# An attention loop's context products gathered from two visits of 32 passes into one of 64

## The reference

```python
q, k, v = (proj(Wq, bq), proj(Wk, bk), proj(Wv, bv))     # 8 heads of 32
scores = jnp.einsum('bhqd,bhkd->bhqk', q, k) * SCALE
scores = scores * (adj_matrix + bond_matrix)[:, None, :, :]
attn = jax.nn.softmax(scores, axis=-1)
ctx = jnp.einsum('bhqk,bhkd->bhqd', attn, v)
ctx = ctx.transpose(0, 2, 1, 3).reshape(b, seq_len, EMBED_DIM)
return jnp.einsum('bse,fe->bsf', ctx, Wo) + bo
```

## Time and profile before

| | us |
|---|---|
| median of 3 runs | 3239.82 |
| lowest, highest | 3238.65, 3240.64 |
| profiled execution | 3240.96 |
| its span, first to last instruction | 3239.2 |
| TensorE busy | 3078.7 |
| VectorE busy | 2119.0 |
| ScalarE busy | 1710.0 |
| POOL busy | 444.6 |

### The profile page before, as it was taken

The page is one execution under the profiler, slowest core; times in us unless marked ns, Lnnn a source line. Parts: engine busy times, 40 slices in busy tenths (PEclk is TensorE's granted clock), DMA queues, the critical chain, the costliest instruction groups (busy, mean ns, idle before and its releaser), DMA issues.

```text
span 3239.2 us, 71078 instructions
## 1 busy us (share of the span) xinstructions
PE 3078.7 (95%) x28440; PEld 2706.9 (84%) x28440; DVE 2119.0 (65%) x3844; ACT 1710.0 (53%) x2945; POOL 444.6 (14%) x1666
## 2 busy tenths in 40 slices
PE   7999999999999998999989999899998999989999
PEld 6988789887898788987789877898778987789877
DVE  5636976279762797627966279663886538875388
ACT  3425854258442684426844268442784327743277
POOL 0001210012100121001211012111121111211112
PEclk9999999999999999999999999999999999989999
DMA  5022131121311213212133021330213302133020
GB/s 211 26 80 63 48 141 48 58 69 44 138 59 50 66 51 131 79 33 67 47 131 98 16 70 43 129 105 12 68 51 121 105 14 68 53 117 105 17 47 19
DMA packets 145270, 234.51 MB, mean 72 GB/s; under 512 B 12840, under 2 KB 113965, under 8 KB 144941
## 3 DMA queue, kind: packets, MB, share of 16 engines
q1 hardware_dynamic: 144940, 229.96, 22.0%
HBM read 120.86 MB, written 83.89 MB: 63 GB/s over the span
## 4 chain that ended last, share of the span: by engine, by line
PE 84%; DVE 10%; ACT 3%; issue 1%; SPq 1%; POOL 1%; DMA 0%; DVEq 0%; POOLq 0%; ACTq 0%
PE ps L463 15%; PE ps L465 15%; PE ps L464 15%; PE ps L661 14%; PE ps L651 9%; PE ps L679 7%; DVE rsum L1172 2%; PE ps L543 2%; PE ps L597 1%; PE ps L518 1%; DVE xt_lo L1093 1%; PE ps L532 1%; PE ps L692 1%; SPq L366 1%; DVE al_area L1206 1%
## 5 line engine op out<-in xcount | busy, mean ns | idle before, releaser
L1328 DVE CUSTOM_DVE_ANT_0 r<-ps,adjn 128x1024 f32<-128x1024 f32 x512 | 620.7, 1212 | 20.9 <-DVE xr L1364 11.3
L1037 ACT ACTIVATE r<-r,nmax 128x1024 f32<-128x1024 f32 x512 | 585.3, 1143 | 23.7 <-POOL nmax L455 22.6
L463 PE MATMUL ps<-u_hi,t_hi 128*128 128x256 f32 x2048 | 590.3, 288 | 5.3 <-DVE u_lo L1086 4.8
L464 PE MATMUL ps<-u_lo,t_hi 128*128 128x256 f32 x2048 | 581.5, 284 | 0.0
L465 PE MATMUL ps<-u_hi,t_lo 128*128 128x256 f32 x2048 | 581.2, 284 | 0.0
L661 PEld LDWEIGHTS ps<-ident,r 128*128 128x128 f32 x4096 | 461.5, 140 | 116.1 <-issue 77.6
L661 PE MATMUL ps<-ident,r 128*128 128x128 f32 x4096 | 537.0, 274 | 7.4 <-DVE pt L1344 7.2
L1344 DVE COPY pt<-ps 128x512 f32<-128x512 f32 x512 | 353.0, 689 | 93.1 <-PE ps L661 71.3
L463 PEld LDWEIGHTS ps<-u_hi,t_hi 128*128 128x128 f32 x2048 | 394.3, 193 | 9.8 <-DVE u_lo L1086 6.4
L836 ACT ACTIVATE pt<-ps 128x512 f32<-128x512 f32 x512 | 304.2, 594 | 176.0 <-PE ps L661 157.7
L464 PEld LDWEIGHTS ps<-u_lo,t_hi 128*128 128x128 f32 x2048 | 395.0, 193 | 0.0
(11 more groups left out here) (157 smaller groups left out, 5282.4 us busy)
## 6 DMA issues: line engine op xcount, KB each, us to landing
adjn<-in_adj SPq DMA_DIRECT2D x64, 512.0 KB, 3.5
t_spill<-t_hi SPq DMA_DIRECT2D x64, 512.0 KB, 4.1
t_spill<-t_lo SPq DMA_DIRECT2D x64, 512.0 KB, 5.1
t_hi<-t_spill SPq DMA_DIRECT2D x32, 1024.0 KB, 5.3
t_lo<-t_spill SPq DMA_DIRECT2D x32, 1024.0 KB, 8.2
xn<-in_x SPq DMA_DIRECT2D x16, 512.0 KB, 4.6
x_spill<-xn SPq DMA_DIRECT2D x64, 128.0 KB, 1.7
q_stack<-u_hi SPq DMA_DIRECT2D x64, 128.0 KB, 2.4
```

Source lines behind the costliest of these rows:

```text
L463: pe.matmul(dst, a_hi, b_hi, start=first, stop=False, skip_group_check=check)
L464: pe.matmul(dst, a_hi, b_lo, start=False, stop=False, skip_group_check=check)
L1037: act.activation(r[:, s % RSLOTS, :], r[:, s % RSLOTS, :], ACT.Exp, bias=nmax[:, s % 4:s % 4 + 1], accum_out=prow[:, qt % 2, h:h + 1]).the ...
L1328: dve.tensor_tensor_reduce(out=r[:, s % RSLOTS, :], in0=ps[:, 2 * (s % 2):2 * (s % 2) + 2, :].rearrange("p a c -> p (a c)"), in1=adjn[:, q ...
```

## The change

It calls `context` once for each group, at s = 4 grp + 8, with all eight key tiles (64 weight loads and 64 passes), waiting for both engines' copies. `ctx_half` goes; VectorE's copy waits for `ctx_done`. The spread moves one step earlier, to 8 qt + 11, the output product one step later, to 8 qt + 17. With the output, these move one step later: VectorE's residual sum and statistics, POOL's `norm_tile`, ScalarE's normalisation. The diff:

```diff
--- before.py
+++ after.py
@@ -253,7 +253,6 @@
         p_full = sem("p_full")
         p_act = sem("p_act")
         p_dve = sem("p_dve")
-        ctx_half = sem("ctx_half")
         ctx_done = sem("ctx_done")
         rp_ready = sem("rp_ready")
         rbc_full = sem("rbc_full")
@@ -435,9 +434,9 @@
                 layer_norm(b, 0)
                 for layer in (1, 2):
                     layer_norm(b, layer)
-                for u in range(UNITS + 13):
-                    if u >= 20 and (u - 20) % H == 0 and (u - 20) // H < NT:
-                        norm_tile(b, 3, (u - 20) // H)
+                for u in range(UNITS + 14):
+                    if u >= 21 and (u - 21) % H == 0 and (u - 21) // H < NT:
+                        norm_tile(b, 3, (u - 21) // H)
                     if u >= 16 and (u - 16) % H == 0 and (u - 16) // H < NT - 1:
 
                         qt = (u - 16) // H
@@ -662,24 +661,22 @@
                                             r[:, u % RSLOTS, (TPH * half + t) * P:(TPH * half + t + 1) * P], ident)
                     last.then_inc(p_full, 1)
 
-            def context(b, grp, part):
+            def context(b, grp):
 
                 qt, g = divmod(grp, 2)
-                if part == 0:
-                    pe.wait_ge(p_dve, nth(b, UNITS, G * grp + G))
-                    if grp == 0:
-                        pe.wait_ge(pr_free, nth(b, PR_UNITS, PR_UNITS))
-                    elif g == 0:
-                        pe.wait_ge(c_raw, nth(b, NT, qt))
-                else:
-                    pe.wait_ge(p_act, nth(b, UNITS, G * grp + G))
-                for kt in range(TPH * part, TPH * (part + 1)):
+                pe.wait_ge(p_dve, nth(b, UNITS, G * grp + G))
+                if grp == 0:
+                    pe.wait_ge(pr_free, nth(b, PR_UNITS, PR_UNITS))
+                elif g == 0:
+                    pe.wait_ge(c_raw, nth(b, NT, qt))
+                pe.wait_ge(p_act, nth(b, UNITS, G * grp + G))
+                for kt in range(NT):
                     for hh in range(G):
                         h = g * G + hh
                         last = pe.matmul(ps[HD * hh:HD * (hh + 1), 6, g * P:(g + 1) * P],
                                          xn[:, kt, h * HD:(h + 1) * HD], p_half(grp * G + hh, kt // TPH)[:, kt % TPH, :],
                                          start=(kt == 0), stop=(kt == NT - 1), tile_position=(0, HD * hh))
-                last.then_inc(ctx_done if part else ctx_half, 1)
+                last.then_inc(ctx_done, 1)
 
             def spread_denominators(b, qt):
 
@@ -821,14 +818,13 @@
                         project_pairs(b, "values", W_V, xt_wait(b, 3), range(s, s + 1))
                     if LAG <= s < UNITS + LAG:
                         transpose_p(b, s - LAG)
-                    for part in range(2):
-                        grp, late = divmod(s - 7 - 2 * part, G)
-                        if late == 0 and 0 <= grp < 2 * NT:
-                            context(b, grp, part)
-                    if s >= 12 and (s - 12) % H == 0 and (s - 12) // H < NT:
-                        spread_denominators(b, (s - 12) // H)
-                    if s >= 16 and (s - 16) % H == 0 and (s - 16) // H < NT:
-                        output(b, (s - 16) // H)
+                    grp, late = divmod(s - 8, G)
+                    if late == 0 and 0 <= grp < 2 * NT:
+                        context(b, grp)
+                    if s >= 11 and (s - 11) % H == 0 and (s - 11) // H < NT:
+                        spread_denominators(b, (s - 11) // H)
+                    if s >= 17 and (s - 17) % H == 0 and (s - 17) // H < NT:
+                        output(b, (s - 17) // H)
 
 
         @block.scalar
@@ -1017,9 +1013,9 @@
                     act.activation(qk_place(part, u_hi, qk0_hi), ps[:, PR + n % 2, :], ACT.Identity,
                                    bias=cols[:, 2 + m, ft:ft + 1]).then_inc(qk_hi, 1)
                 stacks_copied(range(G, 4 * G, 2))
-                for s in range(UNITS + 14):
-                    if s >= 21 and (s - 21) % H == 0 and (s - 21) // H < NT:
-                        normalise(b, 3, (s - 21) // H)
+                for s in range(UNITS + 15):
+                    if s >= 22 and (s - 22) % H == 0 and (s - 22) // H < NT:
+                        normalise(b, 3, (s - 22) // H)
                     if LAG <= s < UNITS + LAG:
                         u = s - LAG
                         if u == 0:
@@ -1316,7 +1312,7 @@
                                              scalar=cols[:, 2 + m, ft:ft + 1], in1=f32(qk_place(part, u_hi, qk0_hi)),
                                              op0=ALU.add, op1=ALU.subtract).then_inc(pr_free, 1)
                 stacks_copied(range(G + 1, 3 * G + 2, 2))
-                for s in range(UNITS + 13):
+                for s in range(UNITS + 14):
                     if s < UNITS:
                         qt, h = divmod(s, H)
                         dve.wait_ge(s_full, nth(b, UNITS, s + 1))
@@ -1340,7 +1336,7 @@
                                 dve.wait_ge(stacked[g], nth(b, 16 * 6, 16 * 6))
                         dve.wait_ge(p_full, nth(b, 2 * UNITS, 2 * u + 1))
                         if u >= P0SLOTS:
-                            dve.wait_ge(ctx_half, nth(b, 2 * NT, (u - P0SLOTS) // G + 1))
+                            dve.wait_ge(ctx_done, nth(b, 2 * NT, (u - P0SLOTS) // G + 1))
                         dve.tensor_copy(p_half(u, 0).rearrange("p t q -> p (t q)"), ps[:, TP, :]).then_inc(p_dve, 1)
                     if s >= 8 and (s - 8) % H == 0 and (s - 8) // H < NT:
                         qt = (s - 8) // H
@@ -1357,8 +1353,8 @@
                     if s == H * (NT - 1) + 15:
                         dve.wait_ge(c_hi_ready, nth(b, NT, NT))
                         rest(c_lo[:, :, :], c_f[:, :, :], c_hi[:, :, :], c_ready)
-                    if s >= 17 and (s - 17) % H == 0 and (s - 17) // H < NT:
-                        qt = (s - 17) // H
+                    if s >= 18 and (s - 18) % H == 0 and (s - 18) // H < NT:
+                        qt = (s - 18) // H
                         dve.wait_ge(o_full, nth(b, NT, qt + 1))
                         dve.wait_ge(xr_biased, nth(b, NT, qt + 1))
                         dve.tensor_tensor(xr[:, qt % 2, :], ps[:, 7, 0:F], xr[:, qt % 2, :],
@@ -1366,8 +1362,8 @@
                         dve.wait_ge(h_sum, nth(b, NT, qt + 1))
                         if qt == NT - 1:
                             dve.sem_inc(drained, 1)
-                    if s >= 18 and (s - 18) % H == 0 and (s - 18) // H < NT:
-                        tile_stats(b, 3, (s - 18) // H)
+                    if s >= 19 and (s - 19) % H == 0 and (s - 19) // H < NT:
+                        tile_stats(b, 3, (s - 19) // H)
 
 
 # ---- launch: one core; inputs and outputs as the reference has them ----
```

## The result

| | us, median | lowest, highest | ratio to before, 95% interval |
|---|---|---|---|
| before | 3239.83 | 3238.65, 3240.64 | |
| after | 3307.31 | 3302.14, 3313.65 | 1.0209 (1.0191 to 1.0228) |

The change made the kernel 67.5 us slower. 3304 us was forecast. The profiled execution took 3308.51 us, its span 3306.7.

A forecast was written before the change was run, and what follows sets the result against it. TensorE's work fills visit steps; light steps take 1.48 us singly, 1.75 in a row at VectorE's pace. Per element +7.6 - 0.8 + 1.2 gives +8.0, 64 us for eight: 3304 us, range 3264 to 3324.

The forecast's parts named there:

- The mechanism: Attention loop: a single light step between visits takes 1.48 us; from the second in a row VectorE's mask-copy order makes it 1.75.
- The price of the merged visit: Context visit of 64 passes on TensorE: 1.89 us, against 2.02 for two visits of 32.
- The 0.41 saved per group: TensorE time per merged visit: 0.13 us from the visit itself, 0.18 at transposes, 0.10 at scores; lower bound 0.31.
- The group with xr and the spread: Steps 0 to 3 modulo 8, with visit, output, residual sum and spread: 9.34 us visit to visit, spread hidden with 0.27 spare.
- t1 to t4: Starts of the transposes in steps with s = 1 to 4 modulo 8: forecast 2.46, 4.51, 5.99, 8.37 us.
- ScalarE's lateness: Rbc and normalisation before ScalarE's copy of step 6 delay the second half of step 7's transposes, to 7.67 from 7.06 us.
- that first rival: Loop slower but ScalarE not late: 18.1 us per row tile, +37 us in all, 3277 us; chance 0.20.
- the walk's own 8.91: Start of step 0's transposes, counted from step 4's, with c_f waiting for rbc to about 6.60 us: 8.91 us.
- The end of an element: From the transposes of unit 61 to the last output, 9.8 us before: +1.2 us.
- The spread's wait for the residual sum: Spread waits for h_sum of the tile before: xr ends about 6.2, spread starts at 7.0, so zero, 0.8 us spare.
- The sum for one element: Per batch element: +7.6 us over 6.9 row tiles, -0.8 at the start, +1.2 at the end, together +8.0.
- The waits priced at zero: New waits for ScalarE's copy and ctx_done, and moved POOL norm_tile and SP stores: no time lost.

The follow-up runs named there:

- the lightened kernels: Mask and exponential on 512 of 1024 columns: kernel before 3227.38 us, changed kernel 3231.82 us, changed kernel with ScalarE's normalisation at 8 qt + 25 3220.64 us.
- the kernel with the moves alone: Kernel before, visits of 32 kept, with spread at 11, output at 17 and its followers one step later: 3265.43 us, ratio 1.0077.
- the run with the moved normalisation: Changed kernel with ScalarE's normalisation at 8 qt + 25 in place of 8 qt + 22, in the long visit's shadow: 3296.74 us.
- the kernel with merging alone: Changed kernel with spread, output and their followers left where the kernel before has them: 3392.93 us, ratio 1.0483.

## Why the prediction was right

The mechanism. A step between visits costs 1.48 only once; the next ones go at VectorE's 1.75. Right for this order: the timeline has 1.47, 1.74, 2.20, and the lightened kernels show it from the other side. As a general price it fails in one place: in the kernel with the moves alone a single light step took 1.97, since VectorE came to it late, behind the residual sum and the statistics.

The price of the merged visit: 1.89 forecast, 1.89 measured. The 0.41 saved per group was not seen as time, as forecast, except where the other engines have room.

The group with xr and the spread: from t1 to t4 every step is as forecast, within 0.01 us. The spread was hidden as said.

ScalarE's lateness: the place was right (rbc and the normalisation ahead of the copy of step 6), its size was not. The visit of step 0 started 1.19 us behind its transposes, forecast 1.27, and moving the normalisation gave 0.18 us per row tile. The prediction held 0.4 us for it, by setting 18.5 beside 18.1. The step that failed is in that first rival: it let c_f run without its wait for rbc (8.75 for t0), and this wait stays wherever the normalisation is. With the walk's own 8.91 the rival would have been 18.25, as the run with the moved normalisation had it (18.23), 0.30 below the walk's 18.55. Measured were 0.18 us per row tile and 10.6 us in all, not the 27 between forecast and rival.

The end of an element: 9.8 to 11.6 us, +1.8 where +1.2 was forecast. The spread's wait for the residual sum was priced at zero with 0.8 us to spare. That holds within the loop, where scores and transposes lie between the two. At the end there are none, and the spread waited 0.61 us, about as much as the term was short; no run took this wait away by itself.

The sum for one element. In the first element the loop from unit 6 to unit 61 went from 118.7 us (307.51 to 426.21) to 125.7 (308.55 to 434.27). On the mean of the eight elements it is +6.8 where +7.6 was forecast (the walk's 9.21 + 9.34 is 18.55, so its own sum would have been +7.9), the start (from unit 0 to unit 6) -0.65 where -0.8 was forecast, the end +1.8 where +1.2 was. That is +8.0, the number forecast, because errors of -0.8, +0.15 and +0.6 cancel: that the total is so close is luck, the steps are not. Eight elements are 64 of the 67.5 us between the profiled executions. Most of the rest lies at the ends of three elements, the third, seventh and eighth. There the granted clock fell to its lower level for 3.4 us, behind unit 61, and these ends took 1.5, 1.5 and 1.7 us longer than the other five, 4.7 us in all. The kernel before has no such stretch from the first unit's transposes to the last's, in any element. Outside the attention loop the changed kernel is 1 us shorter. The sum had no term for the clock; the range had allowed a few us for it.

The waits priced at zero in the steady loop (ctx_done for ctx_half, the visit's wait for ScalarE's copy, POOL, SP) cost TensorE nothing there. ScalarE's exponential stands 0.45 us per row tile for POOL's negated maximum, where it stood 0.34 before; this falls under a visit.

## What to carry to other kernels

Where engines hand units to each other through one or two buffers, lay heavy steps between light ones: a long visit cannot be paid for by light steps behind it, since the other engines cannot work ahead through the visit and then set the pace. Read the price of a light step twice from the trace, once for a single one (1.48 here) and once for the second in a row (1.75), and walk the new order with both before moving work. Walk the other engines as well: their once-a-tile work made a single light step cost 1.97 in the kernel with the moves alone. To save mode changes, put small products of the same mode directly behind each other (spread behind a visit, 12 us) before making the visits longer.

## What the runs showed of the hardware

In the kernel with merging alone, each of five elements has a row tile of over 21 us where 19.90 is usual: one of the first element took 21.36, one of the fifth 23.21. The windows of the first element's slow tile (stretch, its length, busy us and instructions of TensorE, its loads, VectorE, ScalarE, POOL; granted clock; DMA share; GB/s):

```profile
410.00:412.00 2.00, 1.38 (x9) 0.77 (x8) 1.85 (x5) 1.87 (x4) 0.19 (x1) 1.00 0.00 0
412.00:414.00 2.00, 1.17 (x9) 0.72 (x6) 1.90 (x5) 1.24 (x4) 0.48 (x4) 0.95 0.00 0
414.00:416.00 2.00, 2.00 (x10) 1.64 (x8) 1.80 (x4) 0.98 (x2) 0.87 (x3) 0.50 0.03 8
```

The granted clock was at its lower level, 1.2 GHz, from about 414 us on, in the middle of the loop. In the two stretches before, TensorE was busy 1.38 and 1.17 of 2.00 us, and idle in two waits, of 0.62 and 0.83 us. The Trainium skill, "TensorE: Matmul & The Clock Gate", section "HAM oscillation — how this bites in real kernels", speaks of long single waits, for DMA, as what brings the clock down. This trace does not agree in full: the clock fell after two short waits on VectorE, neither over 0.9 us. The same waits stand in every row tile of this kernel, and the clock fell in the middle of the loop only five times, so these waits alone do not settle it. I had not expected a scheduling loss to bring the clock down with it. My estimate of its cost, from the elements with and without such a stretch, is some 10 us of the 23 by which that kernel missed the expectation.

In the changed kernel, whose waits in the loop are shorter, the granted clock of the steady loop was 1.00 in all eight elements. At the loop's end it fell in three of them. The windows of the third element:

```profile
1246.00:1248.00 2.00, 1.16 (x8) 0.68 (x7) 1.92 (x4) 2.00 (x5) 0.19 (x1) 1.00 0.20 66
...
1248.50:1251.90 3.40, 3.40 (x50) 2.74 (x52) 0.90 (x2) 1.83 (x4) 0.43 (x1) 0.50 0.58 193
```

TensorE was busy 1.16 of 2.00 us, and half a microsecond later the clock was at 1.2 GHz. The 64 passes of the visit that follows then took 3.01 us where they take 1.95.
